# A four-layer graph kernel: a norm of node pairs split between ScalarE and VectorE, two scatter rounds moved, the preparation cut in two, a bias carried by the input

## What is computed

```python
x = ln(x + gen(x))     # relu(bn(x)), softmax-weighted sum over edges, W1, LayerNorm, relu, W2, + b2, + x
x = ln(x + gin(x))     # sum over edges, w1, relu, w2, BatchNorm over all rows, relu, + x
x = ln(x + cfconv(x))  # in2f, weights from 20 edge features, sum over edges, o1, softplus, o2
x = ln(x + sage(x))    # two mean aggregations with W1l, W1r, W2l, W2r and biases
```

## Time and profile before

| | |
|---|---|
| median of three runs | 2494.89 us |
| the profiled execution | 2501.6 us, of which the span is 2499.9 us |
| busy over the span | PE 85%, DVE 78%, ACT 72%, POOL 60% |
| setup | 0 to 25.7 us |
| gen_all | 25.7 to 797 us |
| gin | 797 to 1125 us |
| edges_first | 1125 to 1353 us |
| nodes_alone | 1353 to 1797 us |
| edges_middle | 1797 to 2158 us |
| edges_last | 2158 to 2500 us |

### The profile page before, as it was taken

One profiled execution on the slowest core, in us unless ns is written; L12 is line 12 of the kernel. 1 busy time (PEld: TensorE's weight loads), 2 busy tenths in 40 slices (PEclk: granted clock), 3 DMA queues, 4 the chain that ended last, 5 costly groups with the idle time before them and its releaser, 6 DMA issues. The chain is left out here.

```text
span 2499.9 us, 45899 instructions
## 1 busy us (share of the span) xinstructions
PE 2119.8 (85%) x14139; PEld 1774.9 (71%) x14139; DVE 1952.0 (78%) x2832; ACT 1792.0 (72%) x3703; POOL 1506.5 (60%) x1114
## 2 busy tenths in 40 slices
PE   4999999999997999998993886888699999476564
PEld 4999999999996777776772775667566666365553
DVE  5999999999995666668992997889688888387464
ACT  4888888888885677776771886778688998365121
POOL 4788766776621444413555656883068885588787
PEclk9999999999998999998996998999899999788676
DMA  3666665555666888867774676887467886676653
GB/s 104 155 156 156 163 161 151 152 160 159 177 171 168 228 253 253 253 208 197 199 172 88 150 179 148 226 231 194 132 171 208 209 212 189 140 165 152 167 163 92
DMA packets 328930, 438.17 MB, mean 175 GB/s; under 512 B 114943, under 2 KB 170593, under 8 KB 328690
## 3 DMA queue, kind: packets, MB, share of 16 engines
q1 hardware_dynamic: 216386, 377.83, 53.1%
q0 software_dynamic: 112000, 56.93, 13.1%
q10 hardware_dynamic: 304, 0.49, 0.1%
HBM read 244.61 MB, written 191.28 MB: 174 GB/s over the span
## 5 line engine op out<-in xcount | busy, mean ns | idle before, releaser
L1730 POOL DMA_INDIRECT acc<-combined,first_ x100 | 206.0, 2060 | 191.7 <-DMA acc<-combined,first_ 96.2
L454 PE MATMUL banks<-mats,g_hT 128*125 128x256 f32 x1000 | 257.6, 380 | 0.0
L474 PE MATMUL banks<-mats,g_zT 128*125 128x128 f32 x2000 | 238.8, 273 | 0.0
L474 PEld LDWEIGHTS banks<-mats,g_zT 128*125 128x125 f32 x2000 | 228.1, 188 | 0.0
L785 POOL DMA_INDIRECT gin_xs<-x,from_ x100 | 127.0, 1270 | 161.0 <-DMA x_of_src<-gin_xs 137.0
L1790 POOL DMA_INDIRECT combined<-h,from_ x100 | 142.8, 1428 | 121.3 <-PE banks L1888 91.4
L454 PEld LDWEIGHTS banks<-mats,g_hT 128*125 128x125 f32 x1000 | 188.4, 188 | 29.6 <-issue 0.2
L518 ACT ACTIVATE g_sq<-banks 125x512 f32<-125x512 f32 x250 | 148.2, 594 | 82.7 <-PE banks L454 82.1
L591 DVE TENSOR_REDUCE g_ss<-g_sq 125x4 f32<-125x1024 f32 x125 | 151.3, 1210 | 63.9 <-ACT g_sq L518 63.9
L535 ACT ACTIVATE g_zT<-banks,cols 128x500 f32<-128x500 f32 x250 | 179.1, 776 | 1.5 <-PE banks L462 1.5
L953 DVE TENSOR_TENSOR gin_acc<-gin_acc,gin_qr 125x512 f32<-125x512 f32 x125 | 86.7, 694 | 116.4 <-ACT gin_qr L915 116.4
(11 more groups left out here) (395 smaller groups left out, 6656.9 us busy)
## 6 DMA issues: line engine op xcount, KB each, us to landing
acc<-g_zero SPq DMA_DIRECT2D x126, 224.0 KB
x<-g_x SPq DMA_DIRECT2D x125, 224.0 KB
g_x<-in_xT SPq DMA_DIRECT2D x100, 250.0 KB
gin_x<-x SPq DMA_DIRECT2D x50, 448.0 KB
h<-gin_hr SPq DMA_DIRECT2D x50, 448.0 KB
al_h<-h SPq DMA_DIRECT2D x40, 448.0 KB
al_x<-x SPq DMA_DIRECT2D x40, 448.0 KB
out<-al_out SPq DMA_DIRECT2D x40, 448.0 KB
```

What stands on the lines that cost most here:

```text
L454: m = nc.tensor.matmul(bank[0:P, 256 * j:256 * j + 256], HT[q % 2][:, c:c + P], K.W1c, start=False, stop=j == 1)
L474: m = nc.tensor.matmul(pO[q % 2][0:P, D * j:D * j + D], ZT[q % 2][:, h, P * j:P * j + P], K.W2[:, h, :], start=False, stop=j == R - 1 and ...
L1730: pool.indirect_dma_start(out=K.acc, out_offset=bass.IndirectOffsetOnAxis(ap=K.first[:, g, r:r + 1], axis=0), in_=CR[:, g, r * D:r * D + D ...
```

## The change

- **Norm of pairs.** `square_c` squares the first bank (512 columns) as before, and each of the four row blocks of 128 columns of the second with an instruction of its own that also gives the sum (`accum_out`). `reduce_c` sums only the first four rows. `log_c` waits for both. This holds for the 40 pairs of `nodes_alone` and the ten of `edges_last`.
- **Rounds.** `ROUNDS` goes from 13 to 11: two more rounds of additions to `acc` are run by `side` in `nodes_alone`.
- **Preparation in two parts.** `setup` prepares 384 columns of bias rows instead of 640, and does so first. The centring of the four matrix blocks and of two bias rows, `cm`, `bias_s` and `bias_u` move to `Deferred`, whose six pieces VectorE runs in the generator stage at steps 0 to 5, ahead of its other work of the step; SP loads its rows.
- **Bias through x.** `bias_o` and its matrix instruction L468 are gone. `half`, half the centred b2, is added to X: for node groups by a new VectorE instruction `shift` three steps ahead, for edge groups by `own` with a bias. `hidden` takes a corrected offset `ob` and, for a node group, waits for `shift` instead of the DMA. A small TensorE block in `setup` makes `half`.

```diff
+    K.half, K.ob = keep("half", [128, 1]), keep("ob", [128, 1])
...
+        rows_ = tmp("brows", [128, 384])
+        part = [tmp(f"bpart{i}", [128, 384], BF16) for i in range(3)]
+        rest = [tmp(f"brest{i}", [128, 384]) for i in range(2)]
...
+                act.dma_start(rows_[:, :], I["brows"][:, 0:384]).then_inc(rows_in, 16)
...
-                for h in range(4):
-                    nc.scalar.activation(K.bias_o[:, 128 * h:128 * h + 128], K.bias[:, 256:384], ACT.Copy).then_inc(wide, 1)
-                for h in range(4):
-                    nc.scalar.activation(K.bias_s[:, 128 * h:128 * h + 128], K.bias[:, 384:512], ACT.Copy).then_inc(wide, 1)
-                    nc.scalar.activation(K.bias_u[:, 128 * h:128 * h + 128], K.bias[:, 512:640], ACT.Copy).then_inc(wide, 1)
-                act.wait_ge(wide, 14)
+                act.wait_ge(wide, 2)
+
+            @block.tensor
+            def _(pe):
+                pe.wait_ge(cols_in, 16)
+                pe.wait_ge(doubled, 1)
+                nc.tensor.matmul(K.ps[0][:, 0:1], K.twice[:, :], K.c("b2o"), start=True, stop=True).then_inc(centred, 1)
...
+                dve.wait_ge(rows_in, 16)
+                for a, b in ((0, 256), (256, 384)):
+                    link(nc.vector.reduce_sum(mean[:, 0:1], rows_[:, a:b], AX.X))
+                    link(nc.vector.tensor_scalar(mean[:, 1:2], mean[:, 0:1], 1.0 / (b - a), None, ALU.mult))
+                    link(nc.vector.tensor_scalar(rows_[:, a:b], rows_[:, a:b], mean[:, 1:2], None, ALU.subtract))
+                link(nc.vector.tensor_copy(part[0][:, :], rows_[:, :]))
+                link(nc.vector.tensor_tensor(rest[0][:, :], rows_[:, :], part[0][:, :], ALU.subtract))
+                link(nc.vector.tensor_copy(part[1][:, :], rest[0][:, :]))
+                link(nc.vector.tensor_tensor(rest[1][:, :], rest[0][:, :], part[1][:, :], ALU.subtract))
+                link(nc.vector.tensor_copy(part[2][:, :], rest[1][:, :]))
+                dve.wait_ge(consts, 3)
+                link(nc.vector.tensor_scalar(K.bias[:, :], part[0][:, :], K.ident[:, 0:1], None, ALU.mult))
+                for i in (1, 2):
+                    link(nc.vector.scalar_tensor_tensor(out=K.bias[:, :], in0=part[i][:, :], scalar=K.ident[:, i:i + 1],
+                                                        in1=K.bias[:, :], op0=ALU.mult, op1=ALU.add))
+                nc.vector.memset(mean[:, 0:1], 0.0).then_inc(split, 1)
+                dve.wait_ge(split, 1)
+                link(nc.vector.tensor_scalar(K.twice[:, :], K.ident[:, :], 2.0, -2.0 / 128, ALU.mult, ALU.add))
+                nc.vector.memset(mean2[:, 0:1], 0.0).then_inc(doubled, 1)
+                dve.wait_ge(doubled, 1)
                 dve.wait_ge(mats_in, 16)
                 link(nc.vector.reduce_sum(mean[:, 0:1], K.W1c, AX.X))
...
-                cols3 = K.mats[:, 512:1920].rearrange("p (a n) -> p a n", n=128)
-                dve.wait_ge(f1_in, 32)
-                for w, name in enumerate(("o2", "W2lT", "W2rT", "bo2_rows")):
-                    m = K.wi[name] if name in K.wi else 10
-                    link(nc.vector.reduce_sum(mean[:, 0:1], cols3[:, m, :], AX.X))
-                    link(nc.vector.tensor_scalar(mean[:, 1:2], mean[:, 0:1], 1.0 / 128, None, ALU.mult))
-                    link(nc.vector.tensor_scalar(cols3[:, m, :], cols3[:, m, :], mean[:, 1:2], None, ALU.subtract))
...
+                dve.wait_ge(centred, 1)
+                link(nc.vector.tensor_scalar(K.half[:, :], K.ps[0][:, 0:1], 0.25, None, ALU.mult))
+                link(nc.vector.tensor_tensor(K.ob[:, :], K.c("s0"), K.half[:, :], ALU.mult))
+                link(nc.vector.tensor_tensor(K.ob[:, :], K.c("o0"), K.ob[:, :], ALU.subtract))
...
+    def load(self, sp):
+        sp.dma_start(self.rows[:, :], self.K.I["brows"][:, 384:640]).then_inc(self.rows_in, 16)
...
+    def centre(self, dve, block):
+        nc, mean = self.nc, self.mean
+        self.link(dve, nc.vector.reduce_sum(mean[:, 0:1], block, AX.X))
+        self.link(dve, nc.vector.tensor_scalar(mean[:, 1:2], mean[:, 0:1], 1.0 / 128, None, ALU.mult))
+        self.link(dve, nc.vector.tensor_scalar(block, block, mean[:, 1:2], None, ALU.subtract))
+
+    def on_vector(self, dve, n):
+        nc, K, rows, rest, part = self.nc, self.K, self.rows, self.rest, self.part
+        if n == 0:
+            self.centre(dve, K.W("o2"))
+            self.centre(dve, K.W("W2lT"))
+        elif n == 1:
+            self.centre(dve, K.W("W2rT"))
+            self.centre(dve, K.bo2_rows)
+        elif n == 2:
+            dve.wait_ge(self.rows_in, 16)
+            self.centre(dve, rows[:, 0:D])
+            self.centre(dve, rows[:, D:2 * D])
+            self.link(dve, nc.vector.tensor_scalar(K.cm[:, :], K.ident[:, :], 1.0, -1.0 / 128, ALU.mult, ALU.add))
+        elif n == 3:
+            self.link(dve, nc.vector.tensor_copy(part[0][:, :], rows[:, :]))
+            self.link(dve, nc.vector.tensor_tensor(rest[:, :], rows[:, :], part[0][:, :], ALU.subtract))
+            self.link(dve, nc.vector.tensor_copy(part[1][:, :], rest[:, :]))
+            self.link(dve, nc.vector.tensor_tensor(rows[:, :], rest[:, :], part[1][:, :], ALU.subtract))
+            self.link(dve, nc.vector.tensor_copy(part[2][:, :], rows[:, :]))
+        elif n in (4, 5):
+            wide = (K.bias_s if n == 4 else K.bias_u)[:, :].rearrange("p (r d) -> p r d", r=R)
+            part = [p[:, D * (n - 4):D * (n - 3)].rearrange("p (o d) -> p o d", o=1).to_broadcast([128, R, D]) for p in part]
+            self.link(dve, nc.vector.tensor_scalar(wide, part[0], K.ident[:, 0:1], None, ALU.mult))
+            for i in (1, 2):
+                self.link(dve, nc.vector.scalar_tensor_tensor(out=wide, in0=part[i], scalar=K.ident[:, i:i + 1], in1=wide,
+                                                              op0=ALU.mult, op1=ALU.add))
...
+        df = Deferred(nc, K, ctx)
+        shifted = sem("shifted")
...
+                df.load(sp)
...
-                    nc.tensor.matmul(pO[q % 2][0:P, :], K.ones_all[:, 0:P], K.bias_o[:, :], start=True, stop=False)
-                    for j in range(R):
-                        nc.tensor.matmul(pO[q % 2][0:P, D * j:D * j + D], X[q % NX][:, P * j:P * j + P], K.twice[:, :], start=False, stop=False)
+                    for j in range(R):
...
-                        act.wait_ge(x_in[q % NX], landed[q])
+                        past(act, shifted, t)
...
-                    nc.scalar.activation(HT[q % 2][:, :], X[q % NX][:, :], ACT.Relu, bias=K.c("o0"), scale=K.c("s0")).then_inc(hid, 1)
+                    nc.scalar.activation(HT[q % 2][:, :], X[q % NX][:, :], ACT.Relu, bias=K.ob[:, :], scale=K.c("s0")).then_inc(hid, 1)
...
-                    nc.scalar.activation(X[q % NX][:, :], pE[:, 0:G], ACT.Copy).then_inc(xdc, 1)
+                    nc.scalar.activation(X[q % NX][:, :], pE[:, 0:G], ACT.Identity, bias=K.half[:, :]).then_inc(xdc, 1)
...
+                def shift(q, t):
+                    dve.wait_ge(x_in[q % NX], landed[q])
+                    nc.vector.tensor_scalar(X[q % NX][:, :], X[q % NX][:, :], K.half[:, :], None, ALU.add).then_inc(shifted, 1)
...
+                walk(seq, [(0, "all", lambda q: df.on_vector(dve, q)), (-5, "edge", maximum), (1, "all", reduce), (-4, "edge", fall), (4, "all", reduce_o), (-1, "edge", share),
...
+                           (-1, "edge", join), (-3, "node", shift), (4, "all", apply), (-7, "edge", positive), (-8, "edge", runs_of), (-5, "edge", falls),
...
-            self.nc_.square(act, k, self.pC[0:P, :], self.cs, 2)
+            n, nc = self.nc_, self.nc
+            past(act, self.cs, k, 2)
+            past(act, n.summed, k - 1)
+            past(act, n.logged, k - 2)
+            nc.scalar.activation(flat(n.sq_rows[:, 0:R, :]), self.pC[0:P, 0:512], ACT.Square).then_inc(n.squared, 1)
+            for r in range(R, 2 * R):
+                m = nc.scalar.activation(n.sq_rows[:, r, :], self.pC[0:P, D * r:D * r + D], ACT.Square, accum_out=n.s[k % 2][:, r:r + 1])
+            m.then_inc(self.own, 1)
...
         if k < self.count:
+            past(act, self.own, k)
             self.nc_.log(act, k)
...
-            self.nc_.reduce(dve, k)
+            n = self.nc_
+            past(dve, n.squared, k)
+            past(dve, n.logged, k - 2)
+            self.nc.vector.reduce_sum(n.s[k % 2][:, 0:R], n.sq_rows[:, 0:R, :], AX.X).then_inc(n.summed, 1)
...
-        ROUNDS, PAIRS = 13, NG // 2 - LATE
+        ROUNDS, PAIRS = 11, NG // 2 - LATE
```

More of the change, by code:

```diff
@@ L25 @@
         ("beta", "L1_gnn_beta"), ("bf1", "L2_gnn_b_f1"), ("bf2", "L2_gnn_b_f2"), ("bo1", "L2_gnn_b_o1"),
[L26 removed]
+        ("b1l", "L3_gnn_b1l"), ("b2l", "L3_gnn_b2l"), ("b2o", "L0_gnn_b2"), ("t", None)]
 COLS = [n for n, _ in VECS] + ["s0", "o0", "tmp"]
@@ L143, in setup @@
     K.wf1 = keep("wf1", [RBF, 128])
-    K.bias, K.bias_y, K.bias_o = keep("bias", [128, 640], BF16), keep("bias_y", [128, 512], BF16), keep("bias_o", [128, 512], BF16)
```

(3 more changed lines are left out.)

39 lines of the change are left out of this document (21 added, 18 removed).

## The result

The changed kernel takes 2476.44 us in the median of 20 runs, the kernel before 2497.37 in 20 runs beside it. The ratio is 0.9921 with a 95% interval of 0.9905 to 0.9937: 19.7 us faster (16 to 24), where 3.5 were forecast. One run of the kernel before took 2703.97 us and doesn't count in the ratio. The time lies in the predicted range of 2471 to 2508, but outside the forecast's own range of 2482 to 2499. The profiled execution has a span of 2476.0 us instead of 2499.9.

The account below looks back on a forecast made before the run. VectorE was to replace TensorE as the generator's bound, and ScalarE to bound the pairs; -9.2 + 2.5 - 4.3 - 1.5 + 1.0 + 7 + 1.0 = -3.5 us, median 2494.9 to 2491.4, range 2471 to 2508 (forecast's own 2482 to 2499).

Parts of the forecast that it names:

- the head start of the pair stage: Pair stage starts 25.1 us earlier with 11 rounds, then spends that waiting at the same keep.
- Rival 1: Generator: shift nearly always takes 0.79 us and VectorE overruns; stage loses 14.9 us, +16 in total; chance 0.15.
- Rival 2: Generator: TensorE stays the bound, with shift at 0.4 us filling gaps; total -24 us; chance 0.14.
- Setup, -9.2: Setup: less preparation lets the generator's first load go out at 16.4 instead of 25.69 us, gain 9.2 us.
- Deferred pieces, +2.5: Generator steps 0 to 5: 10.5 us of deferred preparation on VectorE mostly finds room; 2.5 us lost (0 to 6).
- Edge-loaded stretch and light steps, -5.8: Generator without L468: 4.3 us gained during edge work with VectorE the bound, 1.5 us in some 7 steps without it.
- Rivals 4 and 5: Pair stage: 4, moved rounds not given back, total -28 us, chance 0.05; 5, slower step everywhere, total +13, chance 0.12.
- Rounds, +1.0: Pair stage: GpSimd's rounds are conserved and gathers start 1.0 us later than before; sum +1.0 us (-3 to +5).
- Norm of pairs, +7: Pair stage: ScalarE becomes the bound at 10.3 us a step, 0.95 more; 7 us lost in 7.5 steps (2 to 13).
- a sign of being wrong: Norm of pairs: the prediction is wrong if accumulator reads cost less than 0.15 us.
- Rival 3: Pair stage: accumulation is cheap; with an 8.5 us step the tail gains 0.5 us a step; total -14; chance 0.08.
- Last ten pairs, +1: Last ten pairs: load waits swallow what square_c adds every other step; 1.0 us lost (0 to 8).

Follow-up runs that it names:

- shift_twice: Changed kernel with a second instruction of the same kind ahead of each shift, written to a spare tile that nothing reads; ratio 1.0013.
- bias_matmul: Changed kernel with the generator's output bias put back as TensorE's matrix instruction and without shift; ratio 0.9977.
- pieces_end: Changed kernel with the six deferred pieces of the preparation run at generator steps 116 to 121 instead of 0 to 5; ratio 0.9945.
- pieces_early: Changed kernel with the first two deferred pieces run together ahead of the third group's shift and each later piece one step earlier; ratio 0.9911.
- rounds13: Changed kernel with 13 rounds of additions in the first edge stage instead of 11; ratio 0.9917.
- late_keeps: Changed kernel with the pair stage's 25 keeps of gathered rows later in the SP queue, at steps 21 to 37 instead of 18 to 32; ratio 0.9797.
- late_keeps13: Changed kernel with 13 rounds in the first edge stage and the keeps at steps 20 to 36; ratio 0.9834.
- old_norm: Changed kernel with the third norm of node pairs as before: one ScalarE square and one VectorE reduction of 1024 columns; ratio 0.9901.
- log_between: Changed kernel with ScalarE's log_a and exp_a placed between the second and third of the four accumulated blocks; ratio 0.9929.
- late_old_norm: Changed kernel with the keeps at steps 22 to 38 and the third norm of pairs as before; ratio 0.9690.
- late_keeps_before: Kernel before the change with only the keeps moved in SP's queue, to steps 20 to 36; ratio 0.9883.

## Why the prediction came out as it did

The sign was right, and so was the largest pair of terms (the head start of the pair stage, given back in it); the size was not: -3.5 us against -19.7. The time is outside the forecast's own range and lies in the stated one because this was widened for rivals 1 and 2, so that part is luck. By the prediction's own terms:

- **Setup, -9.2: -10.1.** The rows landed for a start at 3.63 us, not 5.0; the chain to W2 took 8.7 us, not 8.2; the tail took 2.2, not 2.3, and the barrier 1.0, not 0.9.
- **Deferred pieces, +2.5: 1.1 to 2.2 alone.** The term was about right (the pieces take 12.5 us of VectorE there, not 10.5), but it was costed as if `shift` weren't there. In one queue the two delay the start by 8.4 us. That the wait for a load costs nothing ("issued five steps ahead and needed three ahead") holds in the middle of the stage; at the start no load has been issued early, and the `shift` of the third group held VectorE for 4.91 us.
- **Edge-loaded stretch and light steps, -5.8: -21.1.** The step that failed is the size of `shift`: 0.5 us for what is 0.39 from start to start. 33 of them are 12.9 us, not 16.5, and VectorE's other work took about 0.06 us a group less than in the stretch before (5.53 + 0.31 = 5.84 expected, 247.27/42.8 = 5.78 measured). No run isolates that, but the rows of the same stretch name most of it: VectorE's instructions stood behind 22 gaps of over 0.03 us where it had been 49, so more of them overlap the one ahead (0.03 us a group beyond the overlap of `shift` itself), and the in-place instruction of the earlier trace rows took 0.41 us in the mean and not 0.49 (0.02 us a group). The 1% left for waits was right (2.7 of 250). VectorE is indeed as full as was said, but its need fell to 5.78 us a group beside TensorE's 5.80, where 5.93 had been worked out. Near the point where two engines need the same, an error of 0.15 us a group is the whole gain. The gain itself isn't firm: from the first to the last group it was 738.4 us in all three traces where TensorE alone is full, and 717.2 or 717.3 in four of the seven with the changed kernel's generator, but 721.4, 724.5 and 725.4 in the other three.
- **Rival 2 (-24 in all)** has the better number, with the wrong reason: TensorE isn't alone at the bound, as shift_twice shows. Rival 1 is out: 5 of 100 `shift` were over 0.6 us. Rivals 4 and 5 are out as well: the head start was given back, and the step was 0.35 us longer, not 1.
- **Rounds, +1.0: -4.6** by the pair that is done last under the keeps (number 31: 594.8 us behind the start of edges_first before, 590.3 after). In the other four traces of the same stage (bias_matmul, pieces_end, shift_twice, pieces_early) it was done at 587.8 to 595.3, so the term is -7 to +0.5, and +1.0 wasn't far off. That the rounds are conserved held; they ran at 14.18 us each (14.15 to 14.50 in the other four), where 14.6 with the discount had been taken. rounds13 shows the conservation, and late_keeps with late_keeps13 its cause, the keeps ahead of the loads in SP's queue. The prediction called it GpSimd's rounds that are conserved; they are conserved only as long as SP waits for them.
- **Norm of pairs, +7: +4.6** from pair 31 to the end of the stage, and +2.1 in the other four traces of the same stage. The structure (new `square_c` plus 8.0 to 8.17 us of loop) was right: 1.49 + 8.17 = 9.66, and 9.69 was measured. The term that was mis-sized is the block, 0.25 us and not 0.47. The 0.29 us behind the read in the earlier trace rows weren't the read's cost alone: here the next instruction starts 0.09 us behind it, under the 0.15 us that the prediction gave as a sign of being wrong. From the figures of the Trainium skill, ScalarE: Activation LUTs, What ACT_TABLE_LOAD costs, I estimate 0.20 us for a block without its read. These rows show 0.16 to the read's start and 0.25 with it, so that estimate was nearer than my price. Rival 3, in which the step gets shorter because the accumulation is cheap, did not come: the accumulation is cheap, but the step is the loop's. (Its step would have been VectorE's 8.8 us and not 8.5.) The stalled stretch was misread too: from the first keep, at step 18, to the 25th, at step 32, it is 14 steps and not 15, 11.2 us each, so GpSimd left more room than the 10.4 us said.
- **Last ten pairs, +1: the stage got 0.6 us shorter.** The waits for loads are still there (4.41 us in the row above), as the prediction said; but this stage took 339.9 to 344.3 us in nine traces with the new norm and 337.5 to 347.0 in five with the old, so neither number is told from nothing.

Sum of what was measured: -10.1 - 12.2 - 0.4 - 4.6 + 4.6 - 0.7 - 0.6 = -24.0 in one profiled execution, -19.7 (16 to 24 faster) by the runs. The largest part of the error is the generator's: -12.2 us where -3.3 had been said.

## What to carry to other kernels

Price an instruction by the distance to the start of the next one, and where two engines will need about the same, work out each to a few hundredths of a microsecond before saying which is the bound. A queue that mixes the waits of two chains ties them: look for the place of each wait before moving work across it, since moving the keeps back by three to five steps shortened the pair stage by 37.6 us, more than any part of the change saved. Idle time in the start-up of a pipeline is latency, not room; work goes into a wait that is there anyway, as pieces_early did. And take a second trace of the same program before reading a few microseconds off a stage.

## What the runs showed of the hardware

- **A `shift` is slow at one phase of GpSimd alone.** In the generators of the fourteen traces, 97 of the 1550 instructions like `shift` and the in-place one of the earlier trace rows took over 0.6 us (0.61 to 0.91; the others took 0.40 to 0.57). Every one of them started 0.37 to 0.68 us ahead of the end of a GpSimd indirect DMA instruction and ended 0.22 to 0.25 us behind that end. None of the others began between 0.36 and 0.74 us ahead of one. This is a coincidence in time, seen in every trace; no run changes GpSimd's work to test it. One such pair, of the changed kernel:

```profile
67.54 1.22 POOL L433 DMA_INDIRECT g_xs<-in_x,idx  x1 [0.30 <-issue]
...
68.23 0.75 DVE L668 TENSOR_SCALAR g_x<-g_x,half 128x500 f32<-128x500 f32 x1
```

- **Where two engines were full, the stage's length varied more.** In seven profiled executions whose generator is the same program (changed kernel, old_norm, rounds13, late_keeps, late_keeps13, log_between, late_old_norm) it took 758.3 to 767.9 us. Where TensorE alone is full (before, late_keeps_before, and bias_matmul with its later start) it took 771.9 to 774.4. late_old_norm follows the changed kernel's groups within 0.1 us, late_keeps leaves them in small steps from about the twelfth group on. What decides isn't known; the number of slow `shift`s (3 to 9) doesn't follow the length. Nor is it shown that the two full engines are the cause: gin, which no edit touches, varied by 5 us of 327.
